# Mean squares of the attention output per head: transposes on TensorE and a reduction on VectorE in place of a product with the head selector

## The chip, the cores and the metric

The kernel runs on one core of a Trainium2 chip. The metric is the device time of one execution in microseconds, the median of several runs. The engines named in the profile are PE (TensorE, with its weight loads listed as PEld), DVE (VectorE), ACT (ScalarE), POOL (GpSimd) and SP (SyncE, which issues plain transfers).

## The reference

A small language model tower over 32 sequences of 512 byte tokens, width 128. Tokens are embedded (a byte table and six hashed n-gram tables), go through three layers of retention attention and a feed-forward part, and last through a layer with eight experts, of which each token uses one. The change lies in the attention of the three layers, in the norm that each head's output gets:

```python
def _msr(X, WQ, WK, WV, WG, WO, gnw, gnb, D):
    ...
    Y = jnp.einsum('bnst,bntd->bnsd', A, V)
    Y = jnp.transpose(Y, (0, 2, 1, 3))
    m = Y.mean(-1, keepdims=True)
    v = ((Y - m) ** 2).mean(-1, keepdims=True)
    Yn = ((Y - m) / jnp.sqrt(v + EPS)).reshape(X.shape[0], X.shape[1], H) * gnw + gnb
    G = X @ WG
    return G * jax.nn.sigmoid(G) * Yn @ WO
```

There are four heads of 32 columns (HD = 32), and EPS is 1e-5. The kernel centres the weights of V by head at the start (`centre`, the line with `vmean`), so each head's output has a mean of zero, and `v` is the mean of the squares.

## The kernel before, in words

Two batches of 512 tokens make a pair and are worked on side by side (index `s`). Each batch is cut into halves of 256 tokens, two chunks of 128 (index `h`). So four sequences are in flight, and each goes through 16 pairs of three layers, `attend` and then `feed`: 192 times `attend` in all. Beside them run the embedding of the next pair (`embed`, with gathers on GpSimd) and the routing of the last (`route`). After the 16 pairs the tiles of the experts follow, in a loop.

The order of work is fixed when the program is built. Every engine has its own list of instructions, and carries it out strictly in that order. The functions `attend`, `feed`, `embed` and `route` exist once for each engine; each `yield at("pe ms", ...)` names a point of the work with a due time from the tables `AT` and `FIRST_AT`, and `by_progress` merges the sequences of an engine by these times. Semaphores (`wait_ge`, `then_inc`) hold an instruction back until its input is there. An instruction that waits holds back everything behind it on its engine.

The steps around the change, for one half of one batch in one layer, with the lines of the profile:

1. TensorE writes the attention output, transposed (a row for each of the 128 columns, tokens along the row), into the first 256 columns of PSUM bank `a` ("pe values").
2. ScalarE, "act sq": line 890 squares it into `sq` in SBUF, and line 891 scales a copy of it by `gn_w` into `zp`.
3. TensorE, "pe ms": for each chunk one float32 product of `sq` (stationary) with four columns of the constant `heads` (moving), which gives the sum of the squares of each head, tokens down the partitions, in eight columns of bank `a` (through the helper `mm`, line 1471).
4. VectorE, "dve ms": line 1259 turns the eight columns into mean plus EPS, `ms`.
5. GpSimd, "pool gr": line 795 raises `ms` to the power of -0.5, `gr`.
6. ScalarE, "act spread": line 896 repeats `gr` over the 32 columns of each head, into `xn`.
7. TensorE, "pe rT_y": two transposes of `xn` into the second 256 columns of bank `a` (helper `half_transposes`, line 1492).
8. VectorE, "dve z": lines 1263 and 1264 multiply `zp` by it, add `gn_b` and multiply by the gate `sw`; then TensorE projects with WO ("pe o").

The helper `half_transposes` also serves the two norms of the layer (tile `xn`), the embedding and the routing (tile `side_n`); line 1545 holds the transposes of `qk`. A transpose is a matmul with the tile as the stationary and the identity (`eye`, part of the constants `con`) as the moving operand. The lines 1229 to 1233 are the rotation of `qk` on VectorE, 883 and 885 the copies of its transpose on ScalarE (`qkT`, `qm`), on which the scores on TensorE wait; line 1254 masks the scores. Lines 1328 to 1365 on VectorE belong to the routing and 1192 to 1205 to the embedding.

Of the kernel before, what the change touches and what calls it, by code (L numbers as in the profile page):

```python
# [11 lines left out]
ALU = mybir.AluOpType  # L12
ACT = mybir.ActivationFunctionType
AX_X = mybir.AxisListType.X

P = 128
# [3 lines left out]
HEADS = 4  # L20
HD = H // HEADS
# [5 lines left out]
NG = len(GRAMS)  # L27
HASHES = 25000
E = 8
# [148 lines left out]
EPS = 1e-5  # L178
# [9 lines left out]
def columns(widths):  # L188
# [8 lines left out]
CONST, CONST_COLS = columns([  # L197
    ("cos", CH * 2 * H), ("sin", CH * 2 * H), ("causal", P), ("heads", P), ("eye", P),
    ("before", P), ("gram_scale", NG), ("beyond", NG), ("vocab", 1), ("byte", 1), ("token", CH), ("rank", E),
    ("region", E), ("half", 16), ("tile", 80), ("gram_row", NG),  # L200
    ("parity", 2)])
PARAM, PARAM_COLS = columns([
    ("ln1_w", LAYERS), ("ln1_b", LAYERS), ("ln2_w", LAYERS), ("ln2_b", LAYERS), ("gn_w", LAYERS),
# [7 lines left out]
def constants(n_tokens):  # L211

    c = np.zeros((P, CONST_COLS), np.float32)
    f32 = np.float32
    half = HD // 2
    s = (np.arange(half, dtype=f32) + f32(0.4 * HD)) / f32(1.4 * HD)
    pos = np.arange(S, dtype=f32)
    inv_freq = (f32(1.0) / f32(10000.0) ** (np.arange(half, dtype=f32) / f32(half))).astype(f32)
    ang = (pos[:, None] * inv_freq[None, :]).astype(f32).astype(np.float64)
    scale = s[None, :].astype(np.float64) ** (pos[:, None].astype(np.float64) / 512.0)  # L220
    gammas = (1.0 - np.exp(np.linspace(np.log(1.0 / 32.0), np.log(1.0 / 512.0), HEADS))).astype(f32)
    decay = gammas.astype(np.float64)[None, :] ** pos[:, None].astype(np.float64)
    sign = np.tile([-1.0, 1.0], half)
    cos, sin = np.repeat(np.cos(ang), 2, 1), np.repeat(np.sin(ang), 2, 1) * sign
    up = np.repeat(scale, 2, 1)[:, None, :] * decay[:, :, None]
    both = [(cos[:, None, :] * m, sin[:, None, :] * m) for m in (up, 1.0 / up)]
    for k, name in enumerate(("cos", "sin")):
        t = np.stack([both[0][k], both[1][k]], 1).reshape(CH, P, 2 * H)
        c[:, CONST[name]] = t.transpose(1, 0, 2).reshape(P, -1)
    i = np.arange(P)  # L230
    c[:, CONST["causal"]] = i[None, :] >= i[:, None]
    c[:, CONST["heads"]] = i[None, :] // HD == i[:, None] // HD
    c[:, CONST["eye"]] = np.eye(P)
    c[:, CONST["before"]] = i[:, None] < i[None, :]
    c[:, CONST["gram_scale"]] = [0.5 / (n * NG) for n in GRAMS]
    c[:, CONST["beyond"]] = np.where(i[:, None] > P - np.array(GRAMS)[None, :], NG * HASHES, 0)
    c[:, CONST["gram_row"]] = [k * HASHES for k in range(NG)]
    c[:, CONST["vocab"]] = i[:, None]
    c[:, CONST["byte"]] = i[:, None] % VOCAB
    c[:, CONST["token"]] = i[:, None] + np.arange(CH)[None, :] * P  # L240
    c[:, CONST["rank"]] = E - np.arange(E)
    c[:, CONST["region"]] = np.arange(E) * (n_tokens + TILE)
    c[:, CONST["half"]] = -0.5
    c[:, CONST["tile"]] = np.arange(80)
    c[:, CONST["parity"]] = (i[:, None] // HD) % 2 == np.arange(2)[None, :]
    return c


def tower_program(nc, x, gram_table, layer_w, params, consts, expert_w, out):
# [4 lines left out]
    region = n_tokens + TILE  # L254
# [8 lines left out]
    with ExitStack() as ctx:  # L263
# [30 lines left out]
        def const(name):  # L294
            return con[:, CONST[name]]
# [36 lines left out]
        sq = two(sb, "sq", [P, CH, H])  # L332
        ms = two(sb, "ms", [P, CH * HEADS])
# [82 lines left out]
        def chunks(ap):  # L416
            return ap.rearrange("p (c n) -> p c n", c=CH)
# [45 lines left out]
        ms_p = two(sem, "y_mean_squares_in_psum")  # L463
        y_ms = two(sem, "y_mean_squares_ready")
# [132 lines left out]
        def half_chunks(h):  # L597
            return range(2 * h, 2 * h + 2)


        CS = [slice(2 * h, 2 * h + 2) for h in range(2)]
# [5 lines left out]
        def bank_a(s, h):  # L607
            return bank(s, 2 * h)
# [225 lines left out]
        def _(act):  # L834
            act.wait_ge(s_hash_T, 1)
            for part in (slice(0, PAIR), slice(PAIR, rows)):
                for n in range(2):
                    last = act.activation(win[:, 4 * n:4 * n + 4, part],
                                          bank(1, 2 + n).rearrange("p (w c) -> p w c", w=4)[:, :, part], ACT.Copy)
# [33 lines left out]
            def attend(it, s, l, h):  # L873
                k = it * LAYERS + l
                yield at("act norm1_T", it, s, h, l)
                norm_T(it, s, 2 * l, h, bank_a(s, h), param("ln1_w", l), param("ln1_b", l))
                yield at("act v", it, s, h, l)
                act.wait_ge(proj_p[s], nth(k, 4, 2 * h + 1))
                act.activation(V[s][:, CS[h], :], chunks(bank_a(s, h))[:, 0:2, :], ACT.Copy)
                act.activation(tg[s][:, TS[h]], bank_a(s, h)[:, 2 * P:], ACT.Tanh, scale=0.5).then_inc(tg_s[s], 1)  # L880
                yield at("act qkT", it, s, h, l)
                act.wait_ge(qkT_p[s], nth(k, 2, h))
                act.activation(qkT[s][:, h].rearrange("p a c n -> p (a c n)"), bank_b(s, h), ACT.Copy)  # L883
                for j in range(2):
                    last = act.activation(qm[s][:, h, j, :], bank_b(s, h)[:, 0:2 * P], ACT.Copy,  # L885
                                          scale=const("parity")[:, j:j + 1])
                last.then_inc(qkT_s[s], 1)
                yield at("act sq", it, s, h, l)
                act.wait_ge(y_p[s], nth(k, 2, h))
                act.activation(sq[s][:, CS[h], :], chunks(bank_a(s, h))[:, 0:2, :], ACT.Square)  # L890
                act.activation(zp[s][:, TS[h]], bank_a(s, h)[:, 0:2 * P], ACT.Copy, scale=param("gn_w", l))\
                   .then_inc(y_sq[s], 1)
                yield at("act spread", it, s, h, l)
                n = CH * HEADS // 2
                act.wait_ge(y_r[s], nth(k, 2, h))
                act.activation(xn[s][:, CS[h], :].rearrange("p c (n d) -> p (c n) d", d=HD),  # L896
                               gr[s][:, h * n:(h + 1) * n].unsqueeze(2).to_broadcast([P, n, HD]), ACT.Copy)\
                   .then_inc(y_rb[s], 1)
                yield at("act ss1", it, s, h, l)
                act.wait_ge(y1_s[s], nth(k, 2, h))  # L900
                square_sums(ss, squares, Y1, s, h, n_ss[s][h])
# [88 lines left out]
        def _(dve):  # L990
# [224 lines left out]
            def attend(it, s, l, h):  # L1215
                k = it * LAYERS + l
                cs, ts = CS[h], TS[h]
                a, b = bank_a(s, h), bank_b(s, h)
# [29 lines left out]
                c = h + 1  # L1248
                dve.tensor_tensor(kv[s][:, c, :], kv[s][:, c - 1, :], kv[s][:, c, :], ALU.add).then_inc(kv_s[s], 1)
                for m in range(2):  # L1250
# [5 lines left out]
                n = CH * HEADS // 2  # L1256
                yield at("dve ms", it, s, h, l)
                dve.wait_ge(ms_p[s], nth(k, 2, h))
                dve.tensor_scalar(ms[s][:, h * n:(h + 1) * n], a[:, 2 * P:2 * P + n], 1.0 / HD, EPS, ALU.mult, ALU.add)\  # L1259
                   .then_inc(y_ms[s], 1)  # L1260
                yield at("dve z", it, s, h, l)
                dve.wait_ge(rT_y[s], nth(k, 2, h))
                link(dve.tensor_tensor(zp[s][:, ts], a[:, 2 * P:], zp[s][:, ts], ALU.mult))
# [205 lines left out]
        def _(pe):  # L1469
            def mm(dst, lhsT, rhs, start=True, stop=True):  # L1470
                return pe.matmul(dst, lhsT, rhs, start=start, stop=stop)  # L1471
# [3 lines left out]
            for w in range(8):  # L1475
                last = pe.transpose(bank(1, 2 + w // 4)[:, (w % 4) * P:(w % 4) * P + P], xf[:, w:w + P], eye)
# [13 lines left out]
            def half_transposes(dst, src, h):  # L1490
                for c in half_chunks(h):
                    last = pe.transpose(dst[:, (c % 2) * P:(c % 2 + 1) * P], src[:, c, :], eye)  # L1492
                return last
# [26 lines left out]
            def attend(it, s, l, h):  # L1520
                k = it * LAYERS + l
                a, b = bank_a(s, h), bank_b(s, h)
# [11 lines left out]
                for c in half_chunks(h):  # L1534
                    last = mm(b[:, (c % 2) * 2 * H:(c % 2 + 1) * 2 * H], xT[s][:, chunk(c)], lw[:, l, LW["qk"]])
# [7 lines left out]
                for m in range(2):  # L1543
                    for c in half_chunks(h):
                        last = pe.transpose(b[:, chunk(2 * m + c % 2)], qk[s][:, c, m * H:(m + 1) * H], eye)  # L1545
# [3 lines left out]
                for c in ((0, 1), (2,))[h]:  # L1549
                    last = mm(a[:, chunk(c % 2)], qk[s][:, c, H:2 * H], V[s][:, c, :])  # L1550
# [5 lines left out]
                for i in range(2):  # L1556
                    for r in range(2):
                        part = slice(64 * r, 64 * r + 64)
                        last = mm((a, b)[r][:, i * 2 * P:(i + 1) * 2 * P].rearrange("p (j q) -> p j q", j=2),
                                  qkT[s][part, h, 1, i, :], qm[s][part, h, 0:2, chunk(i)])  # L1560
# [9 lines left out]
                for c in half_chunks(h):  # L1570
                    i = c % 2
                    for n in range(HEADS):
                        d = slice(n * HD, (n + 1) * HD)
                        last = mm(a[d, chunk(i)], V[s][:, c, d], A[s][:, h, n // 2, 2 * i + n % 2, :], False, i == 1)
                last.then_inc(y_p[s], 1)
                yield at("pe ms", it, s, h, l)
                pe.wait_ge(y_sq[s], nth(k, 2, h))
                for c in half_chunks(h):
                    last = mm(a[:, 2 * P + c % 2 * HEADS:2 * P + (c % 2 + 1) * HEADS], sq[s][:, c, :],
                              const("heads").rearrange("p (n d) -> p n d", d=HD)[:, :, 0])  # L1580
                last.then_inc(ms_p[s], 1)
                yield at("pe rT_y", it, s, h, l)
                pe.wait_ge(y_rb[s], nth(k, 2, h))
                half_transposes(a[:, 2 * P:], xn[s], h).then_inc(rT_y[s], 1)
# [170 lines left out]
```

## Time and profile before

| | |
|---|---|
| median of 3 runs | 2427.72 us (2426.78 to 2428.72) |
| profiled execution | 2428.14 us, span of its trace 2426.3 us |
| mean granted clock of TensorE | 0.978 |
| instructions in the trace | 52865 |
| busy on PE, DVE, ACT, POOL | 2233.4, 1887.8, 1580.5, 1764.3 us |

How to read it: the span is cut from one profiled execution; a line such as L1259 is a line of the kernel, and an instruction that a helper issues has the helper's line, so tiles tell such groups apart. Busy time is the time in which at least one instruction of an engine or group was running; an instruction's duration includes its way through the engine, so that consecutive ones overlap, and what one costs the queue is the distance between starts. A float32 product is recorded as two matmuls with two weight loads, a transpose as one of each. The granted clock is a share of 2.4 GHz: 1.00 is 2.4 GHz, 0.50 is 1.2 GHz. The chain of waits follows the work that ended last back through whatever released each step.

### The profile page before, as it was taken

Reading aid. Unit: us, or ns where it says so; the run is one execution under the profiler, and the core shown is the slowest. Engines: PE = TensorE matmul, PEld = TensorE weight load, DVE = VectorE, ACT = ScalarE, POOL = GpSimd, SP = SyncE. Lnnn points to the kernel's source line nnn. Section 1 sums busy time; section 2 is a strip of 40 time slices with the busy share of each in tenths; the row PEclk is TensorE's granted clock in tenths of the full one; section 3 lists DMA queues with packets and bytes.
Section 4 is the critical chain, followed back from the end, with each engine's and each line's share of the span. In section 5 each row is a group of like instructions: output and inputs, shape, how many; then the busy total and the mean of one; then the engine's idle time right before and its main releaser. Section 6 shows DMA issues by size and latency. Waiting matters only on the chain.

```text
span 2426.3 us, 52865 instructions
## 1 busy us (share of the span) xinstructions
PE 2233.4 (92%) x18308; PEld 1950.1 (80%) x18309; DVE 1887.8 (78%) x5669; ACT 1580.5 (65%) x5066; POOL 1764.3 (73%) x1762
## 2 busy tenths in 40 slices
PE   1489999999999999999999999999999999986985
PEld 0368888888888888888888888888888888875874
DVE  5757878888787888888888888887878888766653
ACT  0256677776767676776776777767676777763653
POOL 5687777777777777777787777777777774333777
PEclk9789999999999999999999999999999999997997
DMA  3111111111111111111111111111111111002332
GB/s 122 28 45 34 24 41 28 40 29 41 27 40 28 36 32 37 33 35 37 26 43 26 42 27 40 29 41 27 37 30 37 33 28 55 2 8 75 101 103 69
DMA packets 63522, 98.11 MB, mean 40 GB/s; under 512 B 19108, under 2 KB 41126, under 8 KB 63152
## 3 DMA queue, kind: packets, MB, share of 16 engines
q0 software_dynamic: 33216, 67.44, 10.6%
q1 hardware_dynamic: 30064, 27.53, 4.1%
q8 instruction: 141, 2.31, 0.4%
q14 instruction: 101, 0.83, 0.1%
HBM read 76.63 MB, written 19.17 MB: 39 GB/s over the span
## 4 chain that ended last, share of the span: by engine, by line
PE 75%; POOL 9%; DVE 8%; issue 4%; ACT 3%; DMA 0%; DVEq 0%; POOLq 0%; SPq 0%
PE psum L1471 65%; PE psum L1492 7%; POOL both_grams L760 4%; PE psum L1545 3%; POOL gr L795 3%; POOL out L821 3%; DVE hid L1254 2%; ACT qm L885 1%; ACT qkT L883 1%; ACT xn L896 1%; DVE side_n L1205 1%; DVE qk L1233 0%; DVE hid L1230 0%; DVE qk L1229 0%; POOL rstd L771 0%
## 5 line engine op out<-in xcount | busy, mean ns | idle before, releaser
L760 POOL DMA_INDIRECT both_grams<-gram_table,idx_all x768 | 780.3, 1016 | 188.5 <-issue 183.0
L1471 PE MATMUL psum<-xT,lw 128*128 128x256 f32 x1920 | 481.8, 385 | 0.0
L795 POOL TENSOR_TENSOR gr<-ms,con 128x8 f32<-128x8 f32 x192 | 319.1, 1662 | 137.9 <-DVE ms L1259 133.1
L1471 PE MATMUL psum<-lw,hid 128*128 128x129 f32 x3072 | 391.0, 276 | 3.4 <-ACT hid L915 3.4
L1471 PEld LDWEIGHTS psum<-lw,hid 128*128 128x128 f32 x3072 | 370.9, 192 | 12.9 <-issue 5.6
L771 POOL TENSOR_TENSOR rstd<-ss,con 128x2 f32<-128x2 f32 x320 | 233.9, 733 | 195.1 <-ACT squares L859 192.7
L1471 PEld LDWEIGHTS psum<-xT,lw 128*128 128x128 f32 x1920 | 341.2, 192 | 32.5
L915 ACT ACTIVATE hid<-psum,par 128x256 f32<-128x256 f32 x768 | 307.1, 486 | 43.8 <-PE psum L1471 41.1
L1471 PE MATMUL psum<-lw,xT 128*128 128x256 f32 (+1 forms) x1536 | 287.9, 330 | 6.5 <-ACT xT L871 6.5
L871 ACT ACTIVATE xT<-psum,par 128x256 f32<-128x256 f32 x384 | 213.5, 560 | 119.8 <-PE psum L1492 118.8
L1471 PEld LDWEIGHTS psum<-lw,xT 128*128 128x128 f32 x1536 | 250.0, 192 | 33.0 <-ACT xT L871 7.2
L1254 DVE TENSOR_TENSOR hid<-psum,con 128x512 f32<-128x512 f32 x384 | 249.5, 684 | 27.2 <-PE psum L1471 23.9
L1492 PE MATMUL psum<-con,xn 128*128 128x128 f32 x1152 | 238.5, 289 | 32.0 <-ACT xn L896 16.4
L1471 PE MATMUL psum<-qm,qkT 64*128 64x256 f32 x1536 | 219.7, 405 | 28.9 <-ACT qm L885 17.2
L1492 PEld LDWEIGHTS psum<-con,xn 128*128 128x128 f32 x1152 | 130.6, 147 | 91.8 <-issue 27.1
L865 ACT ACTIVATE xn<-Y,rstd 128x128 f32<-128x128 f32 x384 | 133.0, 396 | 102.1 <-POOL rstd L771 102.1
L883 ACT ACTIVATE qkT<-psum 128x512 f32<-128x512 f32 x192 | 114.5, 596 | 108.9 <-PE psum L1545 107.2
L1471 PEld LDWEIGHTS psum<-qm,qkT 64*128 64x128 f32 x1536 | 133.3, 187 | 64.0 <-ACT qm L885 23.4
L1229 DVE TENSOR_TENSOR qk<-psum,con 128x512 f32<-128x512 f32 x192 | 131.6, 685 | 65.8 <-PE psum L1471 65.7
L859 ACT ACTIVATE squares<-Y 128x129 f32<-128x129 f32 x384 | 116.1, 308 | 97.1 <-DVE Y L1268 97.1
L1205 DVE SCALAR_TENSOR_TENSOR side_n<-both_grams,gate,side_n 128x256 f32<-128x256 f32 x320 | 157.2, 491 | 8.1
L885 ACT ACTIVATE qm<-psum,con 128x256 f32<-128x256 f32 x384 | 160.8, 477 | 0.0
(244 smaller groups left out, 4747.6 us busy)
## 6 DMA issues: line engine op xcount, KB each, us to landing
both_grams<-gram_table,idx_all POOLq DMA_INDIRECT x768
xb<-x SPq DMA_DIRECT2D x32, 256.0 KB, 3.3
idx_all<-routed_rows SPq DMA_DIRECT2D x20, 132.0 KB
er<-routed_rows SPq DMA_DIRECT2D x20, 132.0 KB
both_grams<-routed_rows SPq DMA_DIRECT2D x20, 132.0 KB
qm<-routed_rows SPq DMA_DIRECT2D x20, 132.0 KB
both_grams<-expert_w SPq DMA_DIRECT2D x8, 321.0 KB, 5.2
lw<-layer_w SPq DMA_DIRECT2D x1, 2503.5 KB, 11.9
```

Of the source, the lines that this page charges most:

```text
L760: pool.indirect_dma_start(grams[s][:, g, c, :], None, gram_table, bass.IndirectOffsetOnAxis(ap=idx_all[:, g, at:at + 1], axis=0))\
L771: pool.tensor_tensor(rstd[s][:, CS[h]], ss[s][:, CS[h]], const("half")[:, 0:2], ALU.pow)\
L795: pool.tensor_tensor(gr[s][:, c], ms[s][:, c], const("half")[:, 0:n], ALU.pow).then_inc(y_r[s], 1)
L865: last = act.activation(xn[s][:, c, :], src[s][:, c, 1:WIDE], ACT.Copy, scale=scale[s][:, c:c + 1])
L871: act.activation(xT[s][:, TS[h]], src[:, 0:2 * P], ACT.Identity, bias=b, scale=w).then_inc(xT_s[s][h], 1)
L883: act.activation(qkT[s][:, h].rearrange("p a c n -> p (a c n)"), bank_b(s, h), ACT.Copy)
L885: last = act.activation(qm[s][:, h, j, :], bank_b(s, h)[:, 0:2 * P], ACT.Copy, scale=const("parity")[:, j:j + 1])
L915: last = act.activation(hid[s][:, h, 2 * m + f, :], src[:, f * 2 * P:(f + 1) * 2 * P], ACT.Gelu, bias=param("ffn_b1", l * FB + 2 * m + f))
L1205: last = dve.scalar_tensor_tensor(acc, grams[s][:, g, CS[h], :], gate[:, g:g + 1], acc, ALU.mult, ALU.add)
L1254: dve.tensor_tensor(A[s][:, h, m], chunks((a, b)[m]), causal.unsqueeze(1).to_broadcast([P, HEADS, P]), ALU.mult).then_inc(sc_s[s], 1)
L1471: return pe.matmul(dst, lhsT, rhs, start=start, stop=stop)
L1492: last = pe.transpose(dst[:, (c % 2) * P:(c % 2 + 1) * P], src[:, c, :], eye)
```

## The change

ScalarE now squares `y / sqrt(HD) + sqrt(EPS / HD)` in place of `y`: scale and bias go in front of the square, the bias from a new column `root_eps` of the constants. Summed over the 32 columns of a head whose mean is zero, the mixed terms cancel, and the sum is the mean of the squares plus EPS. On TensorE the squares are not multiplied by the selector but transposed, 128x128 for each chunk, into the second 256 columns of bank `a`. VectorE sums each run of 32 columns with one reduction, 128x256 to 128x8, in place of the multiplication and addition on 128x8. Semaphores, their counts, the tables of due times and the order of the instructions on every engine are as before.

```diff
@@ columns of the constants
-    ("region", E), ("half", 16), ("tile", 80), ("gram_row", NG),
+    ("region", E), ("half", 16), ("root_eps", 1), ("tile", 80), ("gram_row", NG),
@@ constants
     c[:, CONST["half"]] = -0.5
+    c[:, CONST["root_eps"]] = (EPS / HD) ** 0.5
@@ ScalarE, attend
                 yield at("act sq", it, s, h, l)
                 act.wait_ge(y_p[s], nth(k, 2, h))
-                act.activation(sq[s][:, CS[h], :], chunks(bank_a(s, h))[:, 0:2, :], ACT.Square)
+                act.activation(sq[s][:, CS[h], :], chunks(bank_a(s, h))[:, 0:2, :], ACT.Square,
+                               bias=const("root_eps"), scale=float(HD) ** -0.5)
@@ VectorE, attend
                 yield at("dve ms", it, s, h, l)
                 dve.wait_ge(ms_p[s], nth(k, 2, h))
-                dve.tensor_scalar(ms[s][:, h * n:(h + 1) * n], a[:, 2 * P:2 * P + n], 1.0 / HD, EPS, ALU.mult, ALU.add)\
-                   .then_inc(y_ms[s], 1)
+                dve.tensor_reduce(ms[s][:, h * n:(h + 1) * n], a[:, 2 * P:].rearrange("p (n d) -> p n d", d=HD),
+                                  axis=AX_X, op=ALU.add).then_inc(y_ms[s], 1)
@@ TensorE, attend
                 yield at("pe ms", it, s, h, l)
                 pe.wait_ge(y_sq[s], nth(k, 2, h))
-                for c in half_chunks(h):
-                    last = mm(a[:, 2 * P + c % 2 * HEADS:2 * P + (c % 2 + 1) * HEADS], sq[s][:, c, :],
-                              const("heads").rearrange("p (n d) -> p n d", d=HD)[:, :, 0])
-                last.then_inc(ms_p[s], 1)
+                half_transposes(a[:, 2 * P:], sq[s], h).then_inc(ms_p[s], 1)
```

## Rows read from the trace of the kernel before

**Rows 1.** Page, part 1: busy time, share of the span and instructions of each engine.

```profile
PE 2233.4 (92%) x18308; PEld 1950.1 (80%) x18309; DVE 1887.8 (78%) x5669; ACT 1580.5 (65%) x5066; POOL 1764.3 (73%) x1762
```

**Rows 2.** From 400 to 1900 us: busy PE, PEld, DVE, ACT, POOL; granted clock, DMA.

```profile
400.00:1900.00 1500.00, 1482.46 (x12553) 1296.51 (x12551) 1251.39 (x3704) 1062.46 (x3479) 1167.88 (x1161) 1.00 0.13 34
```

**Rows 3.** Page, part 4: the chain that ended last, by engine, by line.

```profile
PE 75%; POOL 9%; DVE 8%; issue 4%; ACT 3%; DMA 0%; DVEq 0%; POOLq 0%; SPq 0%
PE psum L1471 65%; PE psum L1492 7%; POOL both_grams L760 4%; PE psum L1545 3%; POOL gr L795 3%; POOL out L821 3%; DVE hid L1254 2%; ACT qm L885 1%; ACT qkT L883 1%; ACT xn L896 1%; DVE side_n L1205 1%; DVE qk L1233 0%; DVE hid L1230 0%; DVE qk L1229 0%; POOL rstd L771 0%
```

**Rows 4.** Groups by shape on PE: count, busy us, mean ns, idle before.

```profile
L1492 PE MATMUL psum<-con,xn 128*128 128x128 f32 x1152 | 238.5, 289 | 32.0 <-ACT xn L896 16.4 <-DVE xn L1166 6.8 <-ACT xn L865 6.6
...
L1471 PE MATMUL psum<-con,sq 128*128 128x4 f32 x768 | 99.4, 235 | 1.9 <-ACT zp L891 1.9
```

**Rows 5.** Timeline of PE, from two stretches: start, length in us, line, count.

```profile
1009.32 0.39 PE L1492 MATMUL psum<-con,xn 128*128 128x128 f32 x2
1009.54 0.39 PE L1471 MATMUL psum<-qkT,kv 128*128 128x128 f32 x2
...
1010.43 0.44 PE L1492 MATMUL psum<-con,xn 128*128 128x128 f32 x2
1010.71 1.48 PE L1471 MATMUL psum<-lw,xT 128*128 128x256 f32 x8
...
1028.45 1.89 PE L1471 MATMUL psum<-xT,lw 128*128 128x256 f32 x8
1030.18 0.50 PE L1471 MATMUL psum<-con,sq 128*128 128x4 f32 x4
1030.54 0.63 PE L1545 MATMUL psum<-con,qk 128*128 128x128 f32 x4
```

**Rows 6.** Groups by line and shape on DVE.

```profile
L1263 DVE TENSOR_TENSOR zp<-psum,zp 128x256 f32<-128x256 f32 x192 | 80.5, 419 | 28.1 <-PE psum L1492 26.2
...
L1259 DVE TENSOR_SCALAR ms<-psum 128x8 f32<-128x8 f32 x192 | 31.9, 166 | 40.8 <-PE psum L1471 40.8
...
L1109 DVE TENSOR_REDUCE lw<-lw 128x1 f32<-128x128 f32 x3 | 0.9, 286 | 0.1
...
L1109 DVE TENSOR_REDUCE par<-par 128x3 f32<-128x384 f32 x1 | 0.5, 547 | 0.0
```

**Rows 7.** Waits: who waited for whom, us in total, times, longest.

```profile
POOL gr L795 <- DVE ms L1259: 133.1, 89, 6.6
...
PEld psum L1492 <- ACT xn L896: 23.4, 23, 5.1
...
PE psum L1492 <- ACT xn L896: 16.4, 7, 4.9
```

**Rows 8.** The chain in order of time around 1030 us: start, us, what.

```profile
1030.72 0.17 DVE ms L1259
...
1030.96 1.65 POOL gr L795
...
1033.10 0.44 PE psum L1492 x2
```

**Rows 9.** The chain from 1064 to 1072 us, its first and last piece on DVE.

```profile
1064.79 1.27 DVE hid L1254 x2
...
1071.58 0.09 DVE ms L1259
```

**Rows 10.** Groups by line and shape on ACT.

```profile
L891 ACT ACTIVATE zp<-psum,par 128x256 f32<-128x256 f32 x192 | 90.4, 471 | 0.0
...
L890 ACT ACTIVATE sq<-psum 128x256 f32<-128x256 f32 x192 | 72.5, 378 | 33.6 <-PE psum L1471 33.5
```

**Rows 11.** Timeline of PE near 2193 us, and busy time and clock beside.

```profile
2193.00 3.76 PE L1471 MATMUL psum<-xT,lw 128*128 128x256 f32 x8
...
2196.55 1.07 PE L1471 MATMUL psum<-lw,zp 128*128 128x129 f32 x4
...
2194.00:2196.00 2.00, 2.00 (x6) 1.64 (x5) 1.67 (x6) 0.84 (x2) 0.00 (x0) 0.50 0.49 128
```

## The prediction

> **What bounds the kernel now.** I read the busy shares first, then the middle of the run, the chain of waits, the groups on each engine, and last the timeline around the changed step. The busy shares put TensorE ahead at 92% of the span, VectorE at 78% [rows 1]. In the stretch from 400 to 1900 us, where all four sequences of half pairs are in flight, TensorE is busy 1482.46 of 1500 us at a granted clock of 1.00, and VectorE 1251.39 us, 83% [rows 2]. That alone would say "TensorE, and nothing else". The chain that ended last is more careful: 75% of it is TensorE, but 9% is GpSimd, 8% VectorE and 3% ScalarE, and `POOL gr L795`, the power that follows the changed step, holds 3% [rows 3]. So TensorE's order of work is mostly full, and at some points it waits for a result that came round by another engine. A saving on TensorE counts where the chain runs through TensorE; an addition on VectorE counts where the chain runs through VectorE, or through the step that hands on to `gr`.
>
> **The change, part by part.** Each item happens 192 times: 16 batches, two halves, three layers, two chunks at a time.
>
> *TensorE.* Removed are two float32 products of four columns, which the trace records as four matmuls with four weight loads (768 in 192 groups); added are two transposes, recorded as one matmul and one load each (1152 records for the 576 transposed pairs of `xn`) [rows 4]. What a group occupies is the distance from its start to the next group's start, not its duration, since ends overlap. The group of `sq` starts at 1030.18 and the next at 1030.54: 0.36 us. A pair of transposes in a filled queue goes from 1009.32 to 1009.54, 0.22 us; a slower one goes from 1010.43 to 1010.71, 0.28 us [rows 5]. The saving is 0.36 - 0.22 = 0.14 us each, and 192 x 0.14 = 26.9 us in all. If every new pair cost 0.28 us, it would be 0.08 us each, 15.4 us. I take 0.14, because the work just before this step fills the queue in the same rows. On the path lies the chain's share of TensorE, 75%: **-20.2 us** (bounds 0.75 x 15.4 = -11.5 and the whole -26.9).
>
> *VectorE.* Removed is a `TENSOR_SCALAR` of 128x8, 166 ns; added is a `TENSOR_REDUCE` that reads 128x256 from PSUM and writes 128x8. No reduction of that size is in the trace. Its neighbours take 286 ns over 128 elements and 547 over 384; half way between lies 416 ns for 256. These read SBUF; `zp L1263`, which takes in 128x256 from PSUM, needs 419 ns, so PSUM should add nothing that counts [rows 6]. So each `ms`, 166 ns so far, grows by 250 ns, 48.0 us of VectorE time in all (bounds: 286 - 166 = 120 ns and 547 - 166 = 381 ns each, by which the terms below would be half as large or half as large again). Most of it is hidden, and the waits show by what: of the 192 `gr`, 89 waited for `ms`, and TensorE waited for the spread behind `gr` 23 + 7 = 30 times [rows 7]. In the other cases GpSimd or TensorE was still at earlier work. The chain tells the same with its share: 3% of 2426.3 us is 72.8 us of `gr`, which at 1.65 us each is 44 crossings. One of them stands in the rows: `ms` at 1030.72, `gr`, and TensorE again at 1033.10 [rows 3, 8]. A longer `ms` is paid there: 44 x 0.25 = **+11.0 us**.
>
> Behind `ms` VectorE's queue stands still 0.25 us longer, whatever comes next: the rotation, a mask, the token sums of the next pair. Those who then come late are ScalarE's `qkT` and `qm`, and behind them TensorE's scores. Such a stretch is in the rows too: VectorE holds the chain from the mask at 1064.79 to the `ms` at 1071.58 [rows 9]. VectorE's 8% of the chain are 194 us of its 1887.8 busy us, a tenth [rows 1, 3], so about 20 of the 192 `ms` would fall in such stretches. Some of these end in `gr` and are counted above; I take half of 20 x 0.25: **+2.5 us** (bounds 0 and +5.0).
>
> *ScalarE.* The square gets a bias from a tile and a scale. `sq L890` now takes 378 ns; `zp L891`, as large, with one scale from a tile, 471 [rows 10]. So 93 ns more each, 17.9 us in all. ScalarE is 65% busy and 3% of the chain, 73 of its 1580.5 busy us [rows 1, 3]; the same share of 17.9 is **+0.8 us** (bounds 0 and 17.9 if all were late).
>
> *Free.* The added constant widens a load at the start by one column. The transposes write 256 columns of the bank in place of eight, in the half that the transposed spread overwrites next anyway, behind the same waits. No instruction changes its place in any engine's order, and none is added to GpSimd's or SyncE's queue.
>
> **The sum.** -20.2 + 11.0 + 2.5 + 0.8 = -5.9 us. The profiled execution took 2428.14 us (its span is 2426.3, the rest lies around it), 0.4 above the median of the runs, so it gives 2422.2 against the profiled time and 2421.8 against the median: **2422 us**, 0.24% less. A measurement of this kernel can tell about 0.2% from no change, 4.9 us.
>
> **The rivals.**
> - *The longer `ms` is nearly hidden.* TensorE waited for the spread 30 times only [rows 7]. With 30 x 0.25 = 7.5 us and the whole 26.9 us saved, the time is 2428 - 19 = 2409 us. For it: TensorE busy 99% in the middle [rows 2]. Against it: the chain's 25% outside TensorE, where a saving on TensorE buys nothing.
> - *The gain goes into waits.* When TensorE is earlier and VectorE later, waits that were just met become late. The 20.2 us saved less the 0.8 of ScalarE pay for 19.4 / 0.25 = 78 `ms` on the path; the chain shows 44 to 64, and near 78 the time is that of no change, 2428 us. Or the change doesn't do what it says, and a pair costs 0.28 us: then the sum is -11.5 + 14.3 = +2.8, 2431 us.
> - *VectorE's queue decides, and it is slower.* The place is VectorE between `ms` and the operation TensorE waits for next; the price is 0.25 us a time; it decides from 78 `ms` on the path, and from 97 of them the kernel is slower by over 0.2%. At two thirds, 128, it gives 32.0 - 19.4 = +13 us, 2441 us. For it: VectorE at 83% in the middle, and stretches of 7 us in which it holds the chain [rows 2, 9]. Against it: VectorE stood idle for 40.8 us just before `ms`, waiting for TensorE [rows 6], and such gaps soak up a delay.
> - *The clock falls.* The granted clock is 1.00, the level of 2.4 GHz, through the middle, although 1,152 transposes of `xn` alone stand in the run, spread over its layers [rows 2, 4]. It was 0.50, the level of 1.2 GHz, from 2194 to 2196 us, near the end of the layers [rows 11]. Were transposes to hold the clock up less than products do, 192 fewer groups of products could bring the lower level back. The price is in the rows: eight records of one projection take 1.73 us from start to start at the high level (1028.45 to 1030.18) [rows 5] and 3.55 at the lower (2193.00 to 2196.55) [rows 11]. A tenth of the middle, 150 us, at the lower level would add 150 x (1 - 1.73 / 3.55) = 77 us: 2505 us. The Trainium skill, "TensorE: Matmul & The Clock Gate", "Part 4: PE-mode transpose", says that a transpose does not count as TensorE being busy in the way a product does; by that rule the lower level would come more often after this change. The trace does not bear it out: with that many transposes already there, the middle keeps 1.00.
>
> **How the numbers follow.** The forecast has 0.35, the hidden `ms` 0.12, the gain lost in waits 0.31, VectorE's queue 0.20, the clock 0.02. Faster by over 0.2% are the first two, 0.47; within 0.2% the third, 0.31; slower the last two, 0.22. The range goes down to the 2409 of the first rival and up to 2438, near the 2441 of the third, which leaves out 0.07 or so below and somewhat over 0.1 above. The forecast's own case is 2415 to 2423.
>
> **What would show it.** In the profile after, pairs of transposes from `sq` should lie 0.22 us from the next group, and no matmul of four columns should be left; TensorE's busy time should fall by 20 to 30 us. `ms` should be near 416 ns, with VectorE 48 us busier. `sq` on ScalarE should be near 471 ns. `gr` should keep its 1.66 us and about 3% of the chain. I am wrong if the reduction is much dearer than 416 ns, if TensorE's waits for ScalarE's `qm` or for the spread grow by over 20 us in all (then VectorE's queue hands its delay on), or if TensorE's share of the chain rises and the whole 27 us come back.

## The result, and the profile after

The changed kernel takes 2432.13 us (median of 19 runs, 2430.29 to 2432.99), the kernel before, beside it, 2427.72 us: a ratio of 1.0017, 95% interval 1.001 to 1.0024. It is slower by 4.4 us, a little less than the 4.9 us that the prediction called distinguishable, but 19 runs of each set it apart from no change. The forecast was 5.9 us faster.

The page after the change; its lines answer to [rows 1] and [rows 3]:

```profile
span 2431.2 us, 52097 instructions
PE 2212.8 (91%) x17924; PEld 1905.3 (78%) x17925; DVE 1931.2 (79%) x5669; ACT 1593.9 (66%) x5066; POOL 1772.8 (73%) x1762
PE 54%; POOL 19%; DVE 17%; issue 6%; ACT 3%; DMA 0%; DVEq 0%; POOLq 0%; SPq 0%
PE psum L1473 46%; POOL both_grams L761 7%; PE psum L1494 6%; POOL gr L796 5%; POOL out L822 3%; POOL routed_rows L809 2%; DVE hid L1256 2%; PE psum L1547 2%; DVE ms L1261 1%; DVE qk L1235 1%; DVE hid L1232 1%; DVE qk L1231 1%; POOL rstd L772 1%; DVE side_n L1207 1%; ACT qm L886 1%
```

TensorE did get lighter: 20.6 us less busy, 384 matmul records fewer. VectorE is 43.4 us busier. But TensorE's share of the chain fell from 75% to 54%, VectorE's rose from 8% to 17%, and `gr` from 3% to 5%. The stretch from 400 to 1900 us, against [rows 2]:

```profile
400.00:1900.00 1500.00, 1461.78 (x12224) 1258.79 (x12225) 1279.32 (x3694) 1068.51 (x3462) 1173.47 (x1157) 1.00 0.13 34
```

TensorE is idle for 38.2 us of the 1500 in place of 17.5, at the same granted clock of 1.00. The three changed groups, by line and shape, against [rows 4, 6, 10]:

```profile
L1494 PE MATMUL psum<-con,sq 128*128 128x128 f32 x384 | 75.0, 277 | 1.9 <-ACT zp L893 1.9
L1261 DVE TENSOR_REDUCE ms<-psum 128x8 f32<-128x256 f32 x192 | 80.5, 419 | 28.4 <-PE psum L1494 28.4
L891 ACT ACTIVATE sq<-psum,con 128x256 f32<-128x256 f32 x192 | 90.0, 469 | 34.7 <-PE psum L1473 34.7
```

All three cost what was said: 419 ns for the reduction (416 forecast), 469 for the square (471). The waits, against [rows 7]:

```profile
POOL gr L796 <- DVE ms L1261: 158.2, 130, 6.9
...
PEld psum L1494 <- ACT xn L898: 44.7, 66, 4.9
...
PE psum L1494 <- ACT xn L898: 30.9, 49, 4.7
```

`gr` now waits for `ms` 130 times in place of 89. The two rows of TensorE must not be added: every one of the 49 waits of the matmuls stands at one of the 66 places at which the weight loads wait, and the load's wait there is the same wait, seen from the other queue (at 1077.53 us the loads idle for 0.58 us and the matmuls for 0.39). So TensorE's loads wait for the spread at 66 places in place of 23, and at 49 of them, in place of 7, the matmuls run out of work too, for 30.9 us in place of 16.4. The prediction's 30 times (23 + 7), and the 30 and 115 in the expectations below, count such places twice.

What the matmuls idled for in the stretch from 400 to 1900 us, first before, then after the change:

```profile
PE psum L1471 <- ACT qm L885: 12.4, 24, 0.7
PE psum L1471 <- DVE hid L1254: 2.6, 12, 0.2
...
PE psum L1473 <- ACT qm L886: 12.8, 24, 0.7
PE psum L1494 <- ACT xn L898: 12.1, 35, 0.5
PE psum L1547 <- DVE qk L1235: 6.2, 12, 0.5
PE psum L1494 <- ACT xn L866: 2.7, 12, 0.2
PE psum L1473 <- DVE hid L1256: 2.6, 12, 0.2
```

The added idle time is the spread (12.1 us), the rotation `qk`, which comes from VectorE (6.2), and the transposes of a norm (2.7); before the change none of the three held the matmuls up there. Where the spread's waits are shows in TensorE's timeline; in brackets stands what it idled for. Three stretches from one round of the layers:

```profile
1033.52 0.38 PE L1494 MATMUL psum<-con,sq 128*128 128x128 f32 x2
1033.74 0.60 PE L1547 MATMUL psum<-con,qk 128*128 128x128 f32 x4
...
1036.58 0.44 PE L1494 MATMUL psum<-con,xn 128*128 128x128 f32 x2 [0.46 <-ACT xn L898]
...
1073.25 0.38 PE L1494 MATMUL psum<-con,sq 128*128 128x128 f32 x2
1073.47 1.89 PE L1473 MATMUL psum<-xT,lw 128*128 128x256 f32 x8
...
1077.53 0.44 PE L1494 MATMUL psum<-con,xn 128*128 128x128 f32 x2 [0.39 <-ACT xn L898]
...
1078.74 1.14 PE L1473 MATMUL psum<-qm,qkT 64*128 64x256 f32 x8 [0.33 <-ACT qm L886]
...
1118.71 0.44 PE L1494 MATMUL psum<-con,xn 128*128 128x128 f32 x2 [0.23 <-ACT xn L898]
...
1122.73 1.14 PE L1473 MATMUL psum<-qm,qkT 64*128 64x256 f32 x8 [0.74 <-ACT qm L886]
```

The new pairs take 0.22 us from start to start, as forecast (1033.52 to 1033.74, 1073.25 to 1073.47). The order of work repeats with every pair of batches, and of its twelve `attend` steps these three make TensorE's matmuls wait for the spread. In the kernel before, at the same step as the second, it does not idle; the same transposes follow the feed-forward group without a gap:

```profile
1073.10 1.06 PE L1471 MATMUL psum<-lw,hid 128*128 128x129 f32 x8
1073.99 0.38 PE L1492 MATMUL psum<-con,xn 128*128 128x128 f32 x2
```

### The profile page after: what moved, and what is told of

It reads as the page before. It is cut to its first block, busy times and chain, and to the rows that moved or that the text cites. A ratio compares the mean times of both kernels' runs of the same rounds, so it can differ in the third digit from the quotient of the medians.

```text
span 2431.2 us, 52097 instructions
## 1 busy us (share of the span) xinstructions
PE 2212.8 (91%) x17924; PEld 1905.3 (78%) x17925; DVE 1931.2 (79%) x5669; ACT 1593.9 (66%) x5066; POOL 1772.8 (73%) x1762
## 4 chain that ended last, share of the span: by engine, by line
PE 54%; POOL 19%; DVE 17%; issue 6%; ACT 3%; DMA 0%; DVEq 0%; POOLq 0%; SPq 0%
PE psum L1473 46%; POOL both_grams L761 7%; PE psum L1494 6%; POOL gr L796 5%; POOL out L822 3%; POOL routed_rows L809 2%; DVE hid L1256 2%; PE psum L1547 2%; DVE ms L1261 1%; DVE qk L1235 1%; DVE hid L1232 1%; DVE qk L1231 1%; POOL rstd L772 1%; DVE side_n L1207 1%; ACT qm L886 1%
## 5 line engine op out<-in xcount | busy, mean ns | idle before, releaser
L1473 PEld LDWEIGHTS psum<-lw,hid 128*128 128x128 f32 x3072 | 370.6, 192 | 11.5 <-issue 5.6
L1494 PE MATMUL psum<-con,xn 128*128 128x128 f32 x1152 | 239.0, 290 | 51.8 <-ACT xn L898 30.9
L809 POOL DMA_INDIRECT routed_rows<-row,slot x128 | 136.5, 1067 | 36.1 <-issue 32.5
```

The source lines that it names most:

```text
L809: pool.indirect_dma_start(slots, bass.IndirectOffsetOnAxis(ap=slot[s][:, c:c + 1], axis=0), row[s][:, c, :], None).then_inc(r_done[s], 16)
```

## The experiments

The theory after the result: the prediction's mechanisms were right and two of its sizes were off, because waits multiplied. Two rivals stand for what VectorE's part does: the later end of `ms` (0.25 us, passed on by `gr` and the spread), or VectorE's queue, which stands still as long, so that rotations and masks come late. A third is that TensorE's saving gets nowhere in this order of work. Four runs take the parts one by one.

**ScalarE alone.** The new square, all else as before.

```diff
-                act.activation(sq[s][:, CS[h], :], chunks(bank_a(s, h))[:, 0:2, :], ACT.Square)
+                act.activation(sq[s][:, CS[h], :], chunks(bank_a(s, h))[:, 0:2, :], ACT.Square,
+                               bias=const("root_eps"), scale=float(HD) ** -0.5)
-                dve.tensor_scalar(ms..., a[:, 2 * P:2 * P + n], 1.0 / HD, EPS, ALU.mult, ALU.add)
+                dve.tensor_scalar(ms..., a[:, 2 * P:2 * P + n], 1.0, 0.0, ALU.mult, ALU.add)
```

> ScalarE alone: the square with the bias from a tile and a scale, everything else as before (the product stays on TensorE; VectorE's short step multiplies by 1 and adds 0, at the same cost). The square should take 470 ns in place of 378. If a step in the chain from the attention output to the spread is paid in full wherever TensorE waits for the spread (30 places before), this costs 30 x 0.09 = 3 us or some more, 2430 to 2433 us. If the chain has room there, as the prediction said (+0.8 us), the time stays at 2428 to 2429.

Measured: 2428.78 us against 2428.01, ratio 1.0002 (0.9993 to 1.0011). The square takes 469 ns, and the chain has room for it: +0.8 us, not distinguishable from nothing. It is the size that the prediction gave, but the interval runs from -1.7 to +2.7 us, so that the two agree so closely is luck.

**TensorE alone.** The transposes, with VectorE's short step behind them.

```diff
-                for c in half_chunks(h):
-                    last = mm(a[:, 2 * P + c % 2 * HEADS:...], sq[s][:, c, :], const("heads")...)
-                last.then_inc(ms_p[s], 1)
+                half_transposes(a[:, 2 * P:], sq[s], h).then_inc(ms_p[s], 1)
```

> TensorE alone: the squares are transposed, but VectorE keeps its short step and reads only the first eight columns, so the sum over a head is left out and the values differ. Both theories of the loss (the later end of ms; VectorE's queue standing still) put it behind TensorE and expect here the gain of the prediction's first term, 20 to 27 us, so 2401 to 2408 us, with TensorE waiting for the spread in about 30 places as before. The rival, that the order of work does not let a saving on TensorE through, expects less than 10 us, 2418 us or more.

Measured: 2413.08 us, ratio 0.9938 (0.9924 to 0.9952): -14.9 us, between the two expectations. The saving gets through, but only 14.9 / 26.9 = 55% of it. The transposes themselves are as light as priced: TensorE is busy 2203.8 us in place of 2233.4. Why the rest doesn't come back shows in its middle, with what the matmuls idled for beyond `qm` and the mask:

```profile
PE psum L1492 <- ACT xn L865: 2.7, 12, 0.2
...
PE psum L1492 <- ACT xn L896: 2.4, 12, 0.2
PE psum L1545 <- DVE qk L1233: 1.6, 10, 0.2
...
400.00:1900.00 1500.00, 1475.57 (x12345) 1271.63 (x12344) 1256.31 (x3721) 1069.85 (x3511) 1179.12 (x1171) 1.00 0.13 35
```

No other engine has more to do here than before, and yet TensorE idles 24.4 us of the 1500 in place of 17.5, at three steps where it did not idle before: the transposes of a norm, the spread and the rotation. TensorE alone became earlier and met results that had been ready just in time. The spread is only one of them. In the whole trace its loads wait for the spread 47 times in place of 23, the matmuls 21 times in place of 7, but for 17.9 us in place of 16.4.

**VectorE alone.** A reduction as long as that of the change, behind the old product. The square gets an immediate scale, so that the products give the mean; it takes 379 ns in place of 378.

```diff
-                act.activation(sq[s][:, CS[h], :], chunks(bank_a(s, h))[:, 0:2, :], ACT.Square)
+                act.activation(sq[s]..., ACT.Square, scale=float(HD) ** -0.5)
@@ VectorE
-                dve.tensor_scalar(ms[s][:, h * n:(h + 1) * n], a[:, 2 * P:2 * P + n], 1.0 / HD, EPS, ALU.mult, ALU.add)\
-                   .then_inc(y_ms[s], 1)
+                dve.tensor_reduce(ms[s][:, h * n:(h + 1) * n],
+                                  a[:, 2 * P:2 * P + n].unsqueeze(2).to_broadcast([P, n, HD]),
+                                  axis=AX_X, op=ALU.max).then_inc(y_ms[s], 1)
```

> VectorE alone: TensorE keeps its product, and VectorE runs a reduction as long as that of the change (each of the eight sums read 32 times, the maximum taken, which gives the sum itself; the square has an immediate scale, and EPS is left out). ms should take 415 to 420 ns in place of 166. The prediction's term was +13.5 us, 2441 us. From the waits of the changed kernel (TensorE waits for the spread 115 times in place of 30) I now expect up to 115 x 0.25 = 29 us, so 2441 to 2457 us; under 2436 us neither theory would hold, and the loss would come only together with a faster TensorE.

Measured: 2445.11 us, ratio 1.0066 (1.0053 to 1.008): +17.1 us, above the prediction's 2441 and inside what was expected for it after the result. The reduction takes 420 ns. TensorE's loads wait for the spread 64 times and its matmuls 35 times (23 and 7 before). The last two rows are of the middle alone:

```profile
L1259 DVE TENSOR_REDUCE ms<-psum 128x8 f32<-128x256 f32 x192 | 80.6, 420 | 36.7 <-PE psum L1472 35.5
...
PEld psum L1493 <- ACT xn L896: 37.7, 64, 4.9
PE psum L1493 <- ACT xn L896: 24.9, 35, 4.6
...
PE psum L1493 <- ACT xn L896: 7.4, 23, 0.4
PE psum L1546 <- DVE qk L1233: 4.0, 12, 0.4
```

The three parts add up: 0.8 - 14.9 + 17.1 = +3.0, against +4.4 for the whole; what is left, 1.4 us, is less than the intervals of the two larger parts, about 3 us either way. So the runs don't show that the parts cost more together than apart, nor that they don't.

**The later end of `ms`, or the queue behind it.** VectorE lets `gr` go by a short step and runs the reduction after that, into an added tile `sums`.

```diff
-                dve.tensor_reduce(ms[s][:, h * n:(h + 1) * n], a[:, 2 * P:].rearrange("p (n d) -> p n d", d=HD),
-                                  axis=AX_X, op=ALU.add).then_inc(y_ms[s], 1)
+                dve.tensor_scalar(ms[s][:, h * n:(h + 1) * n], a[:, 2 * P:2 * P + n], 1.0 / HD, EPS, ALU.mult, ALU.add)\
+                   .then_inc(y_ms[s], 1)
+                dve.tensor_reduce(sums[s][:, h * n:(h + 1) * n], sq[s][:, cs, :].rearrange("p c (n d) -> p (c n) d", d=HD),
+                                  axis=AX_X, op=ALU.add)
```

> The changed kernel, but VectorE first runs the short step on eight columns, which releases gr, and only then a reduction of the same size (of the squares in SBUF, into a tile that nobody reads); the sum over a head is left out of what follows. So VectorE's queue stands still as long as in the change or 0.08 us longer, and the end of ms is as early as before. If the later end of ms is what costs (TensorE waiting for the spread), this is faster than the changed kernel by most of the loss, 2403 to 2415 us, with some 30 to 50 waits for the spread. If VectorE's queue is what costs, it stays at 2428 to 2436 us.

Measured: 2424.67 us, ratio 0.9984 (0.9975 to 0.9993), between the two expectations. Each taken against the kernel before beside it, it stands at -3.3 us and the changed kernel at +4.4: the gain of 7.7 us is the later end of `ms`. Against TensorE and ScalarE alone (2428.0 - 14.9 + 0.8 = 2413.9) it loses 10.8 us: that is VectorE's queue. In the middle TensorE idles 30.1 us, after 38.2 in the changed kernel; the matmuls wait less for the spread and `qm`, but now for `kv` and `zp`, which VectorE makes behind it:

```profile
PE psum L1476 <- DVE kv L1246: 5.9, 12, 0.5
PE psum L1550 <- DVE qk L1236: 4.9, 12, 0.4
PE psum L1476 <- DVE zp L1269: 3.8, 12, 0.3
PE psum L1476 <- ACT qm L887: 3.2, 12, 0.3
PE psum L1497 <- ACT xn L899: 3.0, 16, 0.2
```

In the changed kernel `qm` and the spread stand there with 12.8 and 12.1 us, and `kv` and `zp` not at all. VectorE holds 26% of this run's chain, after 17% in the changed kernel.

How the loss is split in the change itself is less sure, since the queue stands still longer in this run. From the start of the step to the start of the next instruction it is 0.08 us in the kernel before (1068.45 to 1068.53), 0.33 in the changed kernel (1074.87 to 1075.20) and 0.40 here (1070.86 to 1071.26, both steps together). If the queue's cost goes with the added time, 0.25 in place of 0.32 us, it is 10.8 x 0.25 / 0.32 = 8.4 us in the change, and the later end of `ms` has the rest of 7.7 + 10.8 = 18.5, that is 10.1. This is an estimate from the two runs. Both rivals hold, with about half each; which is the larger is not shown.

This run and TensorE alone leave out the sum, so their values differ, and with them which expert a token goes to. The difference in time does not come from there: from the last `ms` to the end of the trace it is 237.0 us in the kernel before, 235.4 in the changed kernel, 234.5 with TensorE alone and 235.8 here.

**Moving TensorE's side.** If TensorE comes too early to three places, other work could go ahead there. First two of them, then the third, then the third with the projection behind it:

```diff
-    "pe rT_y": ((24.08, 23.76, 23.24), (23.19, 24.23, 21.95), (24.08, 23.76, 23.24), (23.19, 24.23, 21.95)),
+    "pe rT_y": ((24.08, 23.9, 23.24), (23.19, 24.23, 21.95), (24.08, 23.76, 23.24), (23.19, 24.35, 21.95)),
@@ third place
+    "pe rT_y": ((25.2, 23.9, 23.24), (23.19, 24.23, 21.95), (24.08, 23.76, 23.24), (23.19, 24.35, 21.95)),
@@ third place and projection
-    "pe o": ((25.93, 26.12, 25.97), ...
+    "pe o": ((26.4, 26.12, 25.97), ...
```

> The changed kernel with two places of TensorE's order moved: the transposes of the spread go behind the next step in the first half of the first batch in layer 1 (behind the projection with WO of another sequence) and in the second half of the second batch in layer 1 (behind the first feed-forward product of another sequence). There TensorE stood idle for 0.39 and 0.23 us in each period of the middle (one pair through its layers, 129.5 us), while these steps were ready behind it. If the later end of ms costs because TensorE meets these places too early, the idle time goes and the kernel gains up to 15 x 0.62 = 9 us, 2423 to 2427 us. If VectorE's queue sets the pace, the time stays at 2430 to 2434 us, and the idle time turns up at the scores.

> As the run with two places, and a third: the first half of the first batch in layer 0, where TensorE stood idle for 0.45 us in each period, now takes the scores of another half first. By the theory of the later end of ms it gains up to 15 x 1.07 = 16 us against the changed kernel, 2416 to 2423 us, unless the projection that follows then waits for z; by the theory of VectorE's queue 2430 us or more.

> As the run with three places, and in the third the projection with WO goes behind the second part of a feed-forward product, so that z has its time. If the projection waited for z in the run with three places, this is faster than it by up to 15 x 0.5 = 7 us, 2413 to 2420 us; if not, the same.

> The kernel before the change with the two places moved. TensorE stood idle for nothing at these two places there, so the move should bring nothing by itself: 2426 to 2431 us. If it gains as much here as in the changed kernel, the order was simply improvable there, and the two moves say nothing on the change.

Measured: 2434.97, 2446.74 and 2438.61 us for the changed kernel with two places, three, and three with the projection; 2435.98 us for the kernel before with two (before, beside them: 2427.22). With two places both kernels come out above what was expected of them (at most 2434 us for the changed kernel, 2431 for the kernel before). With three the time lies where the theory of VectorE's queue put it, at 2430 us or more, and the projection waits for `z`. With the projection moved as well it is 8.1 us faster than that, as hoped, but the time misses its range by 19 us. With two places moved, the middle of the changed kernel shows:

```profile
PE psum L1473 <- DVE zp L1266: 7.4, 23, 0.4
PE psum L1473 <- DVE hid L1256: 7.0, 24, 0.4
...
PE psum L1473 <- DVE kv L1245: 5.4, 11, 0.5
PE psum L1494 <- ACT xn L898: 5.0, 11, 0.5
```

The waits for the spread went from 12.1 us to 5.0, as meant, and those for `qm` from 12.8 to 4.5; more than that came back as waits for `zp`, the mask and `kv`: VectorE's `z` needs these transposes, it stands in VectorE's fixed order ahead of `kv` and the masks, and TensorE waits for those. With the third place it is `zp`: 19.1 us of waits, up to 1.0 us each. The control is the telling run. In the kernel before, where nothing idles at these places, the same two moves cost 8.8 us, with new waits for the same three results; in the changed kernel they cost 3.3 (7.7 above the kernel before beside it, of which 4.4 are the change's). So the idle time at the two places was worth 5.4 us, but not to be had by TensorE's order alone.

**Moving VectorE's side.** The token sums of the next pair stand between an `ms` and a rotation at two places. First both went far back, then one of them by a few steps only:

```diff
-    "dve onehot": ((1.4,), (5.36,), (1.4,), (5.36,)),
-    "dve acc2": ((3.43,), (-101.47,), (3.43,), (-101.47,)),
-    "dve acc4": ((9.97,), (7.68,), (9.97,), (7.68,)),
@@ both places, far
+    "dve onehot": ((7.2,), (5.36,), (1.4,), (8.86,)),
+    "dve acc2": ((7.5,), (-101.47,), (3.43,), (-101.47,)),
+    "dve acc4": ((9.97,), (7.68,), (9.97,), (9.0,)),
@@ one place, near
+    "dve onehot": ((2.72,), (5.36,), (1.4,), (5.36,)),
+    "dve acc2": ((3.9,), (-101.47,), (3.43,), (-101.47,)),
```

> The changed kernel with VectorE's order altered at two places: the token sums of the next pair (one-hot and the first products with the gates, 1.0 and 2.4 us, which nobody needs soon) go from just ahead of a rotation to behind the z and the state steps that follow. In the changed kernel they stand on VectorE between an ms and the rotation, and behind the rotation waits another ms. If what costs is VectorE handing its delay on (the queue as much as the later end of ms), the changed kernel gains here: the waits of TensorE for the spread at one place (0.39 us a period) and for qm (0.33 and 0.74 us a period) go, up to 15 x 1.4 = 21 us, 2412 to 2425 us. If the other steps that move with them come late in turn, as the projection did when the spread's transposes were moved, 2430 us or more.

> The kernel before the change with the same two moves on VectorE. TensorE waited for qm there too (12.4 us in the middle), so some gain is to be had here as well: 2415 to 2427 us. The changed kernel with the moves is the better of the two by up to 10 us if VectorE's delay was what spoiled the change; it is the worse by 4 us, as without the moves, if the moves have nothing to do with it.

> The changed kernel with one local exchange in VectorE's order, in layer 1 of the first half of the first batch: the one-hot and the first token sums of the next pair (1.04 us) go from just ahead of a rotation to behind that rotation, the ms and the gate that follow it, and two more sums behind the z that follows. Everything is back in its old place two steps later. That ms then ends some 0.6 us earlier, and the rotation too. If the late end of ms and of the rotation behind it are what the change pays with, TensorE's wait for the spread at this place (0.39 us a period) and for qm behind it (0.33 us a period) go, 15 x 0.7 = 10 us, 2420 to 2426 us, below the kernel before. If the gain goes into other waits, as in the runs with larger moves, 2430 us or more.

> The same exchange in the kernel before. TensorE does not wait for the spread at this place there, but it does for qm behind it, so less is to be had: 2422 to 2428 us. By the theory of the late ms the changed kernel gains more from the exchange than this one, and the difference between the two shrinks from 4 us or turns round; if both gain the same, the exchange has nothing to do with the change.

Measured: the far move 2527.53 us with the change and 2538.64 without (before, beside them: 2426.99); the near one 2442.88 with and 2437.42 without (before: 2428.95). None brings the hoped-for gain. The two of the changed kernel end where their texts put the case that the gain goes into other waits, at 2430 us or more; the two of the kernel before miss their ranges. The far move put the sums ahead of a `z` and a mask that TensorE needs: two of its waits in one round,

```profile
1035.60 0.71 PE L1473 MATMUL psum<-lw,zp 128*128 128x129 f32 x4 [1.69 <-DVE zp L1266]
...
1122.93 0.98 PE L1473 MATMUL psum<-qkT,kv 128*128 128x128 f32 x4 [2.26 <-DVE hid L1256]
```

and the granted clock of its middle fell to 0.98 (0.97 without the change). The near move did what it should at its place: the transposes of the spread, for which TensorE idled 0.39 us at 1077.53 in the changed kernel, follow without a wait. The loss comes six groups later on TensorE:

```profile
1080.75 0.44 PE L1494 MATMUL psum<-con,xn 128*128 128x128 f32 x2
...
1082.00 1.14 PE L1473 MATMUL psum<-qm,qkT 64*128 64x256 f32 x8 [0.36 <-ACT qm L886]
...
1085.70 0.68 PE L1473 MATMUL psum<-qkT,kv 128*128 128x128 f32 x4 [0.86 <-DVE hid L1256]
```

VectorE's work of that stretch is one queue: in the same kernel it waits for TensorE at the rotation `qk`, and from there runs without a gap to the end of the masks `hid`, for the second of which TensorE waits.

```profile
1076.10 0.69 DVE L1231 TENSOR_TENSOR qk<-psum,con 128x512 f32<-128x512 f32 x1 [0.59 <-PE psum L1473]
...
1082.18 0.41 DVE L1265 TENSOR_TENSOR zp<-psum,zp 128x256 f32<-128x256 f32 x1
1082.62 0.48 DVE L1266 SCALAR_TENSOR_TENSOR zp<-zp,par,sw 128x256 f32<-128x256 f32 x1
1083.03 0.42 DVE L1270 TENSOR_TENSOR Y<-psum,X 128x258 f32<-128x258 f32 x1
1083.36 0.99 DVE L1207 SCALAR_TENSOR_TENSOR side_n<-both_grams,gate,side_n 128x256 f32<-128x256 f32 x2
1084.28 1.28 DVE L1256 TENSOR_TENSOR hid<-psum,con 128x512 f32<-128x512 f32 x2
```

With the sums gone from ahead of it, the rotation waited 0.59 us for TensorE's projection, and what VectorE idled there it lacked at the mask. Over the whole middle the matmuls wait 7.6 us for the spread in place of 12.1, but 12.9 for the mask in place of 2.6; in the kernel before, the same move takes the mask from 2.6 to 11.9. In this stretch VectorE sets the pace, though it is busy only 79% of the whole. None of these runs beats the kernel before with the same result; the fastest, TensorE's part alone, leaves out the sum. And the worth of the change hangs on the order around it: with the change minus without is +4.4 us in the order as it stands, -1.0 with two places moved, -11.1 with the far move (at clocks that differ as well), +5.5 with the near one. By the text of the near move's control the difference should have shrunk if the late `ms` at this one place were what the change pays with; it did not.

## Why the prediction was wrong, point by point

- *The unit costs.* Right: a pair of transposes 0.22 us from start to start, the reduction 419 ns, the square 469 ns; TensorE 20.6 us less busy, VectorE 43.4 more (48 forecast). The count of 192 is right too, though not as the text explains it: 16 batches, two halves and three layers would be 96; it is 32 batches, 16 pairs of two.
- *ScalarE, +0.8 us.* Not contradicted: +0.8 measured alone, in an interval that includes zero.
- *TensorE, -20.2 us.* Mis-sized: -14.9 measured alone, inside its bounds (-11.5 to -26.9). The step that failed is "on the path lies the chain's share of TensorE, 75%". That share belongs to the old times. With TensorE's part alone 55% of the saving is paid, since the matmuls idle at the norm's transposes, the spread and the rotation, where they did not idle in the middle before.
- *VectorE, +11.0 and +2.5 us.* Mis-sized the other way: +17.1 measured alone, after 13.5. The step that failed is the term for the queue behind `ms`, "I take half of 20 x 0.25", with its upper bound of 5.0: it measured 10.8 us where the queue stood still 0.32 us longer, by the estimate above about 8.4 in the change. The 20 came from VectorE's 8% of the chain, an old share again; in the run that releases `gr` first it is 26%. The term for the later end of `ms`, 11.0, was near: 7.7 us measured, about 10 by the estimate. The reading beside it, that TensorE waited for the spread 30 times, counts seven places twice.
- *The sum, -5.9 us.* Two errors of 5.3 and 3.6 us, both to the same side, turn it to +3.0; the whole measured +4.4. The measured time, 2432.13, lies in the range, and the rival that describes it is "the gain goes into waits", which ended at 2428 us, with a part of "VectorE's queue decides", which began at 97 `ms` on the path.
- *The clock.* The rival did not come about: the granted clock is 1.00 in the middle with 384 transposes more in the run. The Trainium skill, "TensorE: Matmul & The Clock Gate", "Part 4: PE-mode transpose", says that a transpose does not count as TensorE being busy in the way a product does. The lower level that the prediction drew from it did not come back here. The transposes stand between products, so no run here shows what they would do by themselves.
- *The warning signs.* The text named waits for `qm` or for the spread that grow by over 20 us as the mark of VectorE's queue handing its delay on. For the spread the loads wait 21.3 us more and the matmuls 14.5, which are the same waits. The sign is there on the loads and not on the matmuls, and by the run that releases `gr` first, waits for the spread are the mark of the later end of `ms` rather than of the queue.

## What to carry to other kernels

Shares of a chain of waits price only changes that are small against the slack at the places beside the chain: what makes the bounding engine earlier meets results that were just in time, and what makes another engine later turns waits that were just met into late ones, so here the gain read from the shares came out too large (20.2 us, measured 14.9) and the loss too small (13.5, measured 17.1). Where an order of work is fixed, measure the parts of a trade apart (here -14.9, +17.1 and +0.8 us) before judging the trade. And look for the stretches in which a less busy engine runs without a gap; there its time counts in full, and moving its work only moves the wait.

## What the runs showed that was not expected

VectorE, busy 79% of the span, cost TensorE time by its queue alone: 10.8 us in the run whose `ms` is as short as before. With the far move TensorE's middle, at waits of up to 2.3 us, ran at a mean granted clock of 0.98 in place of 1.00:

```profile
400.00:1900.00 1500.00, 1425.93 (x11618) 1225.26 (x11618) 1221.43 (x3500) 1022.85 (x3301) 1117.29 (x1100) 0.98 0.12 32
```

TensorE idles 74.1 us of this stretch, where the two kernels whose clock stays at 1.00 idle 17.5 and 38.2. So part of the 100 us that the far move costs is the lower level (0.50) coming back; how much was not measured apart.
